# A selective-scan kernel: six rows of C streamed through three tiles, a sixth h tile with sums five chunks behind, a second decay tile

## The reference, cut to what matters

```
dlt, Bm, Cm = split(u @ Wdbc.T)                 # 64, 16 and 16 columns
delta = softplus(dlt @ Wdt.T + bdt)
dA  = exp(delta[..., None] * A)                 # A = -exp(Alog)
dBu = delta[..., None] * Bm[:, :, None, :] * u[..., None]
h_t = dA_t * h_{t-1} + dBu_t
y_t = sum over n of h_t[:, :, n] * C_t[:, n]    # then + u * Dp
```

## Time and profile before

| | |
|---|---|
| median of 3 runs | 3286.95 us (3286.11 to 3287.86) |
| the profiled execution | 3287.22 us |
| its span | 3285.4 us |
| busy, whole span: PE / DVE / ACT / POOL | 3000.4 / 3025.4 / 2690.6 / 2904.5 us |
| DMA | 560.40 MB, 171 GB/s mean |
| scans (DVE) | 1024, 2.26 to 2.28 us each |
| products on POOL | 704, 2.38 us each; B products 512, 2.39 us each |
| mean granted clock of PE | 0.985 |

### The profile page before, as it was taken

One profiled execution on the slowest core, in us unless ns is written; L12 is line 12 of the kernel. 1 busy time (PEld: TensorE's weight loads), 2 busy tenths in 40 slices (PEclk: granted clock), 3 DMA queues, 4 the chain that ended last, 5 costly groups with the idle time before them and its releaser, 6 DMA issues.

```text
span 3285.4 us, 54883 instructions
## 1 busy us (share of the span) xinstructions
PE 3000.4 (91%) x19924; PEld 2380.0 (72%) x19924; DVE 3025.4 (92%) x2008; ACT 2690.6 (82%) x5151; POOL 2904.5 (88%) x1288
## 2 busy tenths in 40 slices
PE   8887999899998999899999999899999999899999
PEld 5766666667677666678778676678778666677789
DVE  2838999999999999999999999999999999999994
ACT  1448999988888999987888999987878999988772
POOL 1528999999999999999999999999999999999993
PEclk9989999999999999999999999999999999999999
DMA  5765334644475334645565334645566333645563
GB/s 222 245 237 175 132 117 137 227 154 163 162 249 205 130 119 135 222 139 167 166 229 201 128 122 136 225 142 162 166 211 220 122 128 130 232 136 163 157 198 111
DMA packets 207054, 560.40 MB, mean 171 GB/s; under 512 B 20201, under 2 KB 66473, under 8 KB 202561
## 3 DMA queue, kind: packets, MB, share of 16 engines
q1 hardware_dynamic: 203424, 538.01, 49.0%
q0 software_dynamic: 2304, 16.78, 1.4%
q10 hardware_dynamic: 1056, 2.10, 0.2%
HBM read 476.19 MB, written 80.63 MB: 169 GB/s over the span
## 4 chain that ended last, share of the span: by engine, by line
PE 41%; ACT 21%; DVE 19%; issue 11%; POOL 1%; DVEq 0%; ACTq 0%; POOLq 0%
PE y L888 12%; DVE hbuf L1326 10%; PE slot L899 8%; ACT abuf L1134 8%; PE mb L969 6%; PE mb L859 5%; DVE slot L1326 5%; ACT slot L1195 4%; PE slot L911 3%; ACT dec L1195 3%; DVE delta L1260 2%; DVE hbuf L1331 2%; PE mb L869 1%; ACT soft L1090 1%; ACT yrd L1125 1%
## 5 line engine op out<-in xcount | busy, mean ns | idle before, releaser
L1239 POOL TENSOR_TENSOR hbuf<-hbuf,cres 128x1024 f32<-128x1024 f32 x704 | 1666.4, 2382 | 145.0 <-DVE hbuf L1326 143.7
L1234 POOL TENSOR_TENSOR bst<-bst,du 128x1024 f32<-128x1024 f32 x512 | 1224.6, 2392 | 47.2 <-DVE du L1270 47.2
L1326 DVE TENSOR_TENSOR_SCAN hbuf<-dec,slot 128x1024 f32<-128x1024 f32 x512 | 1164.8, 2275 | 38.5 <-PE slot L911 25.5
L888 PE MATMUL y<-ident,hbuf 128*128 128x128 f32 x8192 | 1017.8, 273 | 1.7 <-POOL hbuf L1239 1.7
L888 PEld LDWEIGHTS y<-ident,hbuf 128*128 128x128 f32 x8192 | 926.2, 141 | 106.0 <-issue 103.4
L1134 ACT ACTIVATE abuf<-dut,bt 128x128 f32<-128x128 f32 x3072 | 970.6, 390 | 0.0
L1326 DVE TENSOR_TENSOR_SCAN slot<-slot,bst 128x1024 f32<-128x1024 f32 x320 | 728.0, 2275 | 24.1 <-ACT slot L1195 23.1
L1195 ACT ACTIVATE dec<-delta,par 128x1024 f32<-128x1024 f32 x512 | 586.3, 1145 | 185.3 <-DVE hbuf L1326 184.8
L1195 ACT ACTIVATE slot<-delta,par 128x1024 f32<-128x1024 f32 x512 | 568.1, 1110 | 123.3 <-DVE hbuf L1331 110.9
L859 PE MATMUL mb<-xn,wzs 128*128 128x512 f32 x1008 | 478.8, 597 | 58.1 <-DVE delta L1260 43.6
L899 PEld LDWEIGHTS slot<-ident,abuf 128*128 128x128 f32 x3072 | 339.4, 141 | 218.3 <-ACT abuf L1134 131.1
(11 more groups left out here) (157 smaller groups left out, 2306.3 us busy)
## 6 DMA issues: line engine op xcount, KB each, us to landing
bst<-bc_s SPq DMA_DIRECT2D x512, 512.0 KB, 3.9
cres<-bc_s SPq DMA_DIRECT2D x128, 512.0 KB, 6.7
wzs<-wz_s SPq DMA_DIRECT2D x64, 256.0 KB, 4.1
yf_s<-yrd SPq DMA_DIRECT2D x32, 512.0 KB, 5.4
ybuf<-yf_s SPq DMA_DIRECT2D x32, 512.0 KB, 5.0
yg_s<-ybuf SPq DMA_DIRECT2D x31, 512.0 KB, 4.4
si_s<-silu SPq DMA_DIRECT2D x28, 512.0 KB, 6.1
silu<-si_s SPq DMA_DIRECT2D x28, 512.0 KB, 5.4
```

Source lines behind the costliest of these rows:

```text
L888: last = nc.tensor.matmul(y[:, j * P:(j + 1) * P], hbuf[:, q % HR, j * P:(j + 1) * P], ident[:], start=False, stop=(q % N == N - 1), is_tr ...
L1234: nc.gpsimd.tensor_tensor(bst[:, i % BR, :], bst[:, i % BR, :], du[:, k % 2, :], ALU.mult).then_inc(pool_b, 1)
L1239: nc.gpsimd.tensor_tensor(hbuf[:, q % HR, :], hbuf[:, q % HR, :], cres[:, q % N, :], ALU.mult).then_inc(pool_prod, 1)
L1326: nc.vector.tensor_tensor_scan(h[:, ::step], decays[:, ::step], inflows[:, ::step], 0.0, ALU.mult, ALU.add).then_inc(scanned, 1)
```

## The change

- `HR` 5 to 6 and `LAG` 4 to 5: six h tiles, and PE sums chunk q - 5 at step q. `skip_terms` and `copy_y` go with LAG to c = 5. On ACT `copy_y` moves in the step too: it was directly behind the decay; it is now behind the decay, the `scale_half` of the step and `softplus_end`.
- `DECS = 2`: `dec` has two tiles, taken in turn by the A and E chunks; a decay waits for the scan of the A or E chunk two before, not one before.
- `STREAMED = (0, 3, 5, 8, 11, 13)`: these six rows of C no longer stay. They go through three tiles in turn and are loaded anew in every unit. SP issues such a load at step q, behind the product of chunk q - 5. The other ten rows (`KEPT`) stay as before. `cres` shrinks from 16 tiles to 13.
- SP stores y at c = 6, not at c = 5.

```
-HR = 5
-LAG = 4
+HR = 6
+LAG = 5
+STREAMED = (0, 3, 5, 8, 11, 13)
+KEPT = [n for n in range(N) if n not in STREAMED]
+CR = 3
+DECS = 2
...
+        def stream_index(q):
+            return q // N * len(STREAMED) + STREAMED.index(q % N)
+        def wait_c(eng, q):
+            if q % N in STREAMED:
+                eng.wait_ge(cs_in[stream_index(q) % CR], 16 * (stream_index(q) // CR + 1))
+            else:
+                eng.wait_ge(c_in[q % N], 16 * (q // SEQ + 1))
...
+            def load_streamed(i):
+                q = STREAM[i]
+                g = q // SEQ
+                sp.dma_start(cres[:, len(KEPT) + i % CR, :],
+                             scratch["bc"][g % 2, g // 2, N + q % N, :].partition_broadcast(P)).then_inc(cs_in[i % CR], 16)
...
+                    if q >= 5 and (q - 5) % N in STREAMED and stream_index(q - 5) + CR < len(STREAM):
+                        wait_product(sp, q - 5)
+                        load_streamed(stream_index(q - 5) + CR)
...
-                    if c == 5 and k > 0 and not backward(k - 1):
+                    if c == 6 and k > 0 and not backward(k - 1):
                         sp.wait_ge(y_read, k)
...
-                        if before("AE", q) > 0:
-                            act.wait_ge(scanned, TURNED[before("AE", q) - 1] + 1)
-                        decays = dec[:]
+                        if before("AE", q) >= DECS:
+                            act.wait_ge(scanned, TURNED[before("AE", q) - DECS] + 1)
+                        decays = dec[:, before("AE", q) % DECS, :]
...
                     nc.scalar.activation(decays, delta[:, k % 2, :], ACT.Exp, ...)
-                    if c == LAG and k > 0:
-                        copy_y(k - 1)
                     if c in SCALE_STEPS: ...
                             scale_half(N * k + n, h)
                     if k + 1 < NU:
                         if c == 4:
                             softplus_start(k + 1)
                         if c == 5:
                             softplus_end(k + 1)
+                    if c == LAG and k > 0:
+                        copy_y(k - 1)
```

More of the change, by code:

```diff
@@ L518, in inflow_step @@
     return max(POOLED[i - DR] + 1, POOLED[i] // N * N - 2)
+STREAM = [q for q in range(NU * N) if q % N in STREAMED]
 INFLOWS_AT = {q: [i for i in range(DR, len(POOLED)) if inflow_step(i) == q] for q in range(NU * N)}
@@ L533, in ssm_kernel @@
         ident, par = t["ident"], t["par_sb"]
-        cres = sb("cres", [P, N, S])
+        cres = sb("cres", [P, len(KEPT) + CR, S])
         bst, dl, xn, wz, wdt = (t[n] for n in ("bst", "dl", "xn0", "wzs", "wdt"))
@@ L537, in ssm_kernel @@
         delta, du = (sb(n, [P, 2, S]) for n in ("delta", "du"))
-        soft, ud, yrd, silu, ybuf, dec, dut = (sb(n, [P, S]) for n in (
-            "soft", "ud", "yrd", "silu", "ybuf", "dec", "dut"))
+        soft, ud, yrd, silu, ybuf, dut = (sb(n, [P, S]) for n in (
+            "soft", "ud", "yrd", "silu", "ybuf", "dut"))
+        dec = sb("dec", [P, DECS, S])
         abuf = sb("abuf", [P, 2, S])
@@ L554, in ssm_kernel @@
         c_in = [sem(f"c_in{n}") for n in range(N)]
+        cs_in = [sem(f"cs_in{i}") for i in range(CR)]
         last_in = sem("last_in")
@@ L617, in z_bank, with c_tile @@
             return mb[h] if k > 0 else y[:, half(h)]
+        def stream_index(q):
+            return q // N * len(STREAMED) + STREAMED.index(q % N)
+        def c_tile(q):
+            if q % N in STREAMED:
+                return cres[:, len(KEPT) + stream_index(q) % CR, :]
+            return cres[:, KEPT.index(q % N), :]
+        def wait_c(eng, q):
+            if q % N in STREAMED:
+                eng.wait_ge(cs_in[stream_index(q) % CR], 16 * (stream_index(q) // CR + 1))
+            else:
+                eng.wait_ge(c_in[q % N], 16 * (q // SEQ + 1))
         def wait_scanned_out(eng, q):
@@ L694, in load_c @@
             def load_c(g, n):
[L695 removed]
+                sp.dma_start(cres[:, KEPT.index(n), :],
                              scratch["bc"][g % 2, g // 2, N + n, :].partition_broadcast(P)).then_inc(c_in[n], 16)
+            def load_streamed(i):
[3 more added lines that the diff above has]
+                             scratch["bc"][g % 2, g // 2, N + q % N, :].partition_broadcast(P)).then_inc(cs_in[i % CR], 16)
             def load_forward_y(k):
@@ L735, in store_dbc @@
                                  dbc[R:RD, d, :]).then_inc(dbc_out, 16)
-            for n in range(3):
+            load_streamed(0)
+            for n in (1, 2):
                 load_c(0, n)
+            for i in range(1, CR):
+                load_streamed(i)
             for k in range(NU):
@@ L748, in _ @@
                         load_b(before("VP", q - 2) + BR)
-                    if k == 0 and c + 3 < N:
+                    if k == 0 and c + 3 in KEPT:
                         load_c(0, c + 3)
+                    if q >= 5 and (q - 5) % N in STREAMED and stream_index(q - 5) + CR < len(STREAM):
+                        wait_product(sp, q - 5)
+                        load_streamed(stream_index(q - 5) + CR)
                     if k == ET and c == 0:
@@ L789, in _ @@
                     if k == NU - 1 and c >= ET:
-                        wait_product(sp, q - ET)
+                        wait_product(sp, N * k + KEPT[c - ET])
                         sp.dma_start(skip_tile(TAIL + c - ET), scratch["xs"][NC - 2 + (c - ET) // TB, :, c % TB, :]).then_inc(rest_in, 16)
@@ L819, in _ @@
                         load_gated(block_now, yp_in)
-                    if e == ET - 1 and k + 1 < NU and c >= 5:
+                    if e == ET - 1 and k + 1 < NU and c - 5 in KEPT:
                         wait_product(sp, q - 5)
                         load_c(k // ET + 1, c - 5)
-                    if e == 0 and k >= ET and c < 5:
+                    if e == 0 and k >= ET and c < 5 and N - 5 + c in KEPT:
                         wait_product(sp, q - 5)
@@ L1212, in _ @@
                             softplus_end(k + 1)
+                    if c == LAG and k > 0:
+                        copy_y(k - 1)
+                    if k + 1 < NU:
                         if c in (zs + 2, zs + 4):
@@ L1236, in product @@
             def product(q):
-                pool.wait_ge(c_in[q % N], 16 * (q // SEQ + 1))
+                wait_c(pool, q)
                 pool.wait_ge(scanned, q + 1)
-                nc.gpsimd.tensor_tensor(hbuf[:, q % HR, :], hbuf[:, q % HR, :], cres[:, q % N, :],
+                nc.gpsimd.tensor_tensor(hbuf[:, q % HR, :], hbuf[:, q % HR, :], c_tile(q),
                                         ALU.mult).then_inc(pool_prod, 1)
@@ L1318, in _ @@
                         dve.wait_ge(turned, before("AE", q + 1))
-                        decays, inflows = dec, slot[q % 2]
+                        decays, inflows = dec[:, before("AE", q) % DECS, :], slot[q % 2]
                     else:
@@ L1329, in _ @@
                         dve.wait_ge(scanned, q + 1)
-                        dve.wait_ge(c_in[c], 16 * (q // SEQ + 1))
-                        nc.vector.tensor_tensor(hbuf[:, q % HR, :], slot[q % 2][:], cres[:, c, :],
+                        wait_c(dve, q)
+                        nc.vector.tensor_tensor(hbuf[:, q % HR, :], slot[q % 2][:], c_tile(q),
                                                 ALU.mult).then_inc(dve_prod, 1)
```

## The result

The changed kernel takes 3488.17 us (median of 4 runs, 3482.35 to 3498.77) beside 3286.53: 1.0613 times as long, 95% interval 1.0598 to 1.0627. The forecast was 3434 with a range up to 3480; the time lies 8 us above that.

What follows compares the result with a forecast made beforehand. DVE was taken as the bound, with PE a second bound in mx units from the z product to the next unit's chunk 1. 3287.2 + 54 (queue behind the copy) + 93 (clock) = 3434 us, range 3325 to 3480.

Steps and rivals of the forecast that it cites:

- The copy of y and the queue behind it: ACT copies y late; PE's skip, sum and turn queue behind: 1.25 us per mx unit, 0.45 per gating unit, together 54.
- The clock, in mx units: Low clock on PE behind its idle hole costs 1.6 us in each of 32 mx units.
- The clock, in gating units: Low clock on PE behind its idle hole costs 1.4 us in each of 30 gating units.
- C through the ring: Streamed C loads land in time and don't hold up the B load: value 0, ends 0 and 2 us per unit (130).
- The second decay tile: Removes ACT's wait for the scan of the A or E chunk before: value 0, ends 0 and -3.
- the sixth h tile: Gives POOL one chunk more of room, which it doesn't need: value 0.
- long low stretches: Rival: low clock of 6.8 us in most units, losing about 2.8 us per mx, 2 per gating unit; 3491, chance 0.13.
- the one of the streaming: Rival: streaming holds DVE or POOL up, 130 us on top of the 54; 3471, chance 0.04.

Runs made afterwards that it cites:

- stream: Kernel before with only the streaming of six rows of C (five h tiles, LAG 4, one decay tile, copy_y in its old place): 3321.46 us, 1.0103.
- gated_early: Changed kernel with the gated tiles' load issued at step 12 instead of 13, ahead of the B and C loads: 3456.60 us, 1.0494.
- p1: Changed kernel with copy_y directly behind the decay of chunk 5: 3332.15 us, 1.0138 of the kernel before.
- p2: Changed kernel with copy_y behind the scaling of step 5 and ahead of softplus_end: 3400.51 us, 1.0341 of the kernel before.
- p1_early: Changed kernel with copy_y directly behind decay 5 and the gated tiles' load one step earlier: 3297.85 us, 1.0016 of the kernel before.

## Why the prediction was wrong, point by point

- **The copy of y and the queue behind it: right.** ACT's 4.17 us, the hole (forecast 4.0 to 4.6 us, measured 3.9 on average), skip, sum and turn in a row, DVE at chunk 6. Forecast 1.25 us in an mx unit and 0.45 at chunk 6; measured without the clock 1.03 and 0.40. In a projecting unit it is 0.7, not 0.45.
- **The clock, in mx units: right in size, by two errors that cancel.** I took 1.6 us. A low stretch of 3.4 us costs 1.8 and one of 6.8 us 2.7; in the changed kernel none of the 24 regular mx units is without one and 7 have the long one, which makes 1.95 on average (48.68 - 45.70 - 1.03). The queue is 0.2 smaller than I had it. That the 91 us came out is in part luck.
- **The clock, in gating units: too small.** I took 1.4 us. Of the 17 regular projecting units 7 have the short stretch and 10 the long one (wait at chunk 6 1.90 and 3.03 us). Units 9 to 14, which project to B and C instead of the output and all have the short one, are 2.14 longer instead of 1.85.
- **"C through the ring. Value 0": this step failed.** I checked that the C tiles land in time and that B's queue isn't held up, and the range's end was twice the landing time of a C tile. What was late is another load on the same queue: the gated tiles, 1.3 us in a projecting unit of the streaming kernel and 1.8 in one of the changed kernel. Before, it had little slack: in unit 28 it landed at 40.34 us and PE's first matmul on it began at 40.94. Streaming alone costs 34 us, and taking the load forward in the changed kernel gives 32 back, which is 3457 and within the range.
- **The second decay tile, the sixth h tile: right, 0.** No run shows a gain from either.

The sum, in a projecting gating unit: 4.27 measured = 1.85 forecast + 1.28 (stream) to 1.80 (gated_early) for the gated tiles' load + 0.6 to 1.1 that is left, by difference, for the longer low stretches and the longer queue. So of the 55 us that the gating units are above the forecast, 29 to 41 (23 units) are the load, and the rest is the 1.4 us of the clock term and the 0.45 of the queue, both taken too small. Where the low stretches fall within a unit isn't settled; why some are 3.4 and some 6.8 us I didn't test.

The rivals: "long low stretches" gave 3491, 3 us from the measured time, but by luck: it wants 6.8 us in most units, while only 7 of the 24 regular mx units have that, and it has nothing for the load. That rival and the one of the streaming each held a part of the truth; I had treated them as alternatives when both could happen together, and so the range ended below the time.

The Trainium skill, page "TensorE: Matmul & The Clock Gate", section "HAM oscillation — how this bites in real kernels", describes a loop in which a long enough wait brings the low clock back in every round. The trace agrees: a low stretch behind the hole in 62 of 62 units, and 416 us at the low level in the changed kernel against 99 before.

## What to carry to other kernels

When an instruction is moved on one engine's list, look for the engine that has the next waiter at the head of its own list, and add up everything queued behind it; then ask how long the hole is, because a hole of 4 us on TensorE was paid twice here, once as the queue and once as the clock. When loads are added to a shared queue, check the slack of every load already on it, the ones of other stages above all, not only of the new ones and their neighbours. Effects that can happen together belong in one range, added.

## What the runs showed of the hardware

- A low stretch that comes after a hole stretched eight transposes from 0.87 to 1.71 us from start to start. Of the 93 low stretches of the changed kernel 63 last 3.4 us and 28 last 6.8.
- Short holes are not free of it either: with PE waiting 2.2 us in each unit (p1) the core spent 143 us at the low clock, with 3.0 us (p2) 324, with 3.9 us (changed kernel) 416; without the wait (stream) 113. The length of the hole is not all that counts: p1_early, with 2.0 us, has 212.
- With DMA traffic of 222 GB/s (stream) instead of 171 the durations of scans and products stayed as they were (2.28 and 2.38 us), while the mean landing time of the gated tiles' load of 512 KB went from 5.72 to 6.61 us. Whether the traffic or the C load issued just ahead of it does that, no run separates.
